# Attention logits as full-array matmuls of stacked halves, with maxima, exponentials and turned blocks taken bank by bank

## The chip, the core and the metric

The kernel runs on one core of a Trainium2 chip. The time is the device time of one execution in microseconds. The engines are TensorE (PE), VectorE (DVE), ScalarE (ACT), GpSimd (POOL) and SyncE (SP, which issues most DMAs). Each engine works through its own queue of instructions in the written order; a semaphore wait holds everything behind it on that engine.

## What is computed

A batch has 256 tokens of 256 features and 77 context rows; there are 32 batches. Four layers follow one another, each on a layer norm of x and each added to x with a gate: (a) attention without a softmax (relu of q k, relu of the result), (b) a three-layer network with weights of +1 and -1 (256 to 1024 to 1024 to 256), (c) the attention that the change is about, (d) a mixture of 64 experts with top 8 of them per token, besides a shared expert. Layer (c), cut to its core:

```python
qp = jnp.einsum('bld,ed->ble', q, Wq)
idx = jnp.argmax(jnp.einsum('bld,bmd->blm', qp, kv), axis=-1)
mem = jnp.take_along_axis(kv, idx[..., None], axis=1)
mk, mv = jnp.split(jnp.einsum('bld,ed->ble', mem, Wkv), 2, axis=-1)
qh = qp.reshape(b, l, 16, 16).transpose(0, 2, 1, 3)
attn = jax.nn.softmax(jnp.einsum('bhld,bmd->bhlm', qh, mk) / 4, axis=-1)
out = jnp.einsum('bhlm,bmd->bhld', attn, mv)
```

All 16 heads share one key and one value of 16 features. Since mem only repeats rows of the 77 context rows, the kernel takes the logits against the 77 rows, masks the rows that no token chose, and weighs values and denominator with the count of tokens that chose a row.

## The kernel before

Products that need f32 accuracy are made of f16 halves: x = high + low, and a product is high*high + high*low + low*high (`three`, L986). ACT makes the high part while it copies a result out of PSUM, DVE the low part by subtracting.

The loop over batches is a software pipeline. `body(n)` is `first(n)` and `second(n)`, written out separately for each engine, and holds work of five batches at once: layer (a) of m = n+1, layer (b) of n, layers (c) and the start of (d) of c = n-1, the rest of (d) of d = n-2, and scatters of n-3. The order of an engine's work is the order of the calls, and semaphores join the engines. After the batches a second loop runs over the 64 experts; the change doesn't touch it.

The steps that matter here:

- `b_l0`, `b_l1`, `b_l2` (L1062, L1077, L1095) are the matmuls of (b). `b_l1(0)` to `b_l1(7)` are 16 matmuls each, placed as filler between the steps of (c). ACT and DVE follow with the two halves of a result (`b_l0`, `b_l1` at L777, L783, L1576, L1579). `b_l1(0)` waits for `l0_lo` of the fourth `b_l0`.
- `c_lg(r)` (L1136), r = 0 to 3, makes the logits of 128 tokens (t) and 8 heads (half c of the features). It writes both banks of `ps_lg`, four heads of 77 columns in each. For each of four parts (the mask row, keys high with queries high, keys low with queries high, keys high with queries low) there are two matmuls, one for the upper and one for the lower 64 rows of the array. Keys lie in `kb_h`, `kb_l` as blocks of a diagonal (made by POOL in `take_keys`, L577), the mask in `mrow`.
- `c_max(r)` (DVE, L1630) takes the maxima of 8 heads at once, `c_exp(r)` (ACT, L792) eight exponentials into `p32`. `c_pt(k)` (PE, L1154) turns blocks of 128 columns of `p32`: three for even k, two for odd; ACT copies the high part, DVE the low part (L803, L1640). `c_av(r)` (L1176) multiplies with the values, `c_norm` (DVE) divides.
- There is one `p32` and one `pt_h`, `pt_l`: the exponentials of r wait until the blocks of r-1 are turned.
- `transposes(i, ...)` (L994) turns a normalised x for i = 0 to 3: `xn[0]`, `xn[1]`, `xn[2]` and, for i = 3, `xr`. All four, and `c_att`, write the same bank, `ps_tr`, so each waits for the low part of the one before it:

```python
elif i == 1:
    w(pe, tr_lo[3], b - 1)
```

- `ln_norm(1)` (ACT, L734) makes `xn[1]` from `x1`. It waits for `ln_shift(1)` of DVE (L1541), and that for a power made by POOL. In ACT's order it stands behind `tr_high(3)`, in DVE's order `ln_shift(1)` stands behind `tr_low(3)`.
- `d_gu(j)` (L1219) are the gate and up matmuls of the shared expert. They need `tr_lo[3]`.

PE's order in `second(n)` is: a_q, a_kv, c_av(3), a_vals, a_s, c_att, b_l1(6), c_wc, b_l1(7), a_sv, b_l2(0), transposes(3), b_l2(1), d_gu(0), transposes(1), d_gu(1), d_route, d_gu(2), transposes(2), d_gu(3).

Of the kernel before, what the change touches and what calls it, by code (L numbers as in the profile page):

```python
# [8 lines left out]
F16 = mybir.dt.float16  # L9
# [8 lines left out]
P = 128  # L18
# [7 lines left out]
HB = HC // 2  # L26
VW = DH + 1
# [8 lines left out]
NEG = -1e30  # L36
# [6 lines left out]
TURNED = [range(0, 3), range(3, PC)]  # L43
# [50 lines left out]
def build(nc, x, ctxT, maskT, g_xattn, g_ffn, wq0, wk0, wv0, bq0, bk0, bv0, k0, k1, k2, s0, s1, s2,  # L94
          wqT1, wkvT1, wcT1, gates_w, sgu_w, sdown_w, e_wts, out, table):
    es = ExitStack()
    with es:
# [34 lines left out]
        row0 = sb("row0", [P, P], BF16)  # L132
# [4 lines left out]
        halfmask = sb("halfmask", [P, HB])  # L137
        pad_in = sb("pad_in", [P, 1])
# [70 lines left out]
        kr_h, kr_l = sb("kr_h", [P, S2], F16), sb("kr_l", [P, S2], F16)  # L209
        kb_h, kb_l = sb("kb_h", [P, HB, S2], F16), sb("kb_l", [P, HB, S2], F16)  # L210
# [6 lines left out]
        mrow = sb("mrow", [P, HB, S2], BF16)  # L217
# [5 lines left out]
        p32 = sb("p32", [P, PC * P])  # L223
        pt_h, pt_l = sb("pt_h", [P, PC, P], F16), sb("pt_l", [P, PC, P], F16)
# [8 lines left out]
        th = sb("th", [P, IS // P, S])  # L233
        ga = sb("ga", [P, 4, S])
# [61 lines left out]
        cx_ok, kr_hi = sem("cx_ok"), sem("kr_hi")  # L296
# [4 lines left out]
        lg_rdy, z_ok, p_ok = (many(n, 4) for n in ("lg_rdy", "z_ok", "p_ok"))  # L301
# [80 lines left out]
        def _(sp):  # L382
# [45 lines left out]
            sp.wait_ge(consts2, 31)  # L428
# [76 lines left out]
        def _(pool):  # L505
# [1478 lines left out]
```

## Time and profile before

| | |
|---|---|
| median of 3 runs | 1802.12 us (1801.63 to 1804.59) |
| the profiled execution | 1800.24 us, span 1798.5 us |
| PE busy | 1672.4 us (93% of the span) |
| DVE busy | 1315.4 us (73%) |
| ACT busy | 978.5 us (54%) |
| POOL busy | 945.7 us (53%) |
| chain that ended last | PE 75%, DMA 9%, ACT 5%, issue 5%, DVE 3%, POOL 3% |

The profile shows one execution. An engine's busy time is the union of its instructions. Matmuls are pipelined and the profile models their ends, so that a start follows another after less time than one matmul seems to take; the pace of PE is read from the starts. The batches take the first 1580 us or so of the span, the experts the rest.

### The profile page before, as it was taken

How to read it: one execution, taken by the hardware profiler on the slowest of the kernel's cores; microseconds unless marked ns; L12 is line 12 of the kernel's file. 1: busy time of each engine (PE TensorE's matmuls, PEld its weight loads, DVE VectorE, ACT ScalarE, POOL GpSimd, SP SyncE). 2: the span in 40 equal slices, each digit the busy share in tenths (PEclk: the TensorE clock that was granted, in tenths of full speed). 3: DMA queues.
4: the chain of work that ended last, by engine and by line, in shares of the span. 5: the costliest groups of instructions: out<-in, count | busy, mean ns of one | idle time of the engine just before them, and what ended most of it. 6: DMA issues, size and time to landing. Idle time of an engine off the chain costs nothing.

```text
span 1798.5 us, 51473 instructions
## 1 busy us (share of the span) xinstructions
PE 1672.4 (93%) x17308; PEld 1431.1 (80%) x17308; DVE 1315.4 (73%) x4640; ACT 978.5 (54%) x2819; POOL 945.7 (53%) x1507
## 2 busy tenths in 40 slices
PE   5799999999999999999999999999999999558885
PEld 3588888888888888888888888888888887447775
DVE  6477877777777777777778877778777776546564
ACT  3455556665555555565556555555566654324443
POOL 4015555555555555555555555555555554545554
PEclk8899999999999999999999999999999999679998
DMA  7501111111000101100000000000000012148886
GB/s 221 158 15 52 45 36 39 43 46 33 26 25 23 32 15 32 31 22 22 25 28 23 28 21 14 21 23 25 18 24 21 22 52 77 50 118 208 204 204 131
DMA packets 102656, 101.12 MB, mean 56 GB/s; under 512 B 38879, under 2 KB 92073, under 8 KB 102616
## 3 DMA queue, kind: packets, MB, share of 16 engines
q1 hardware_dynamic: 68824, 81.43, 14.9%
q0 software_dynamic: 33792, 19.17, 6.1%
q8 instruction: 22, 0.36, 0.1%
q14 instruction: 18, 0.15, 0.0%
HBM read 51.63 MB, written 111.84 MB: 91 GB/s over the span
## 4 chain that ended last, share of the span: by engine, by line
PE 75%; DMA 9%; ACT 5%; issue 5%; DVE 3%; POOL 3%; POOLq 0%; SPq 0%; ACTq 0%; DVEq 0%
PE bank L1090 21%; PE bank L991 8%; DMA out<-ey,aid 7%; PE bank L1074 6%; PE ps_yo L1106 5%; PE ps_lg L1150 5%; PE ps_yo L991 4%; PE ps_m L991 4%; PE ps_tr L1017 3%; ACT p L800 3%; PE ps_pt L1165 3%; PE ps_lg L991 3%; PE ps_m L1188 2%; POOL table L615 2%; PE ps_pt L991 2%
## 5 line engine op out<-in xcount | busy, mean ns | idle before, releaser
L615 POOL DMA_INDIRECT table<-xs,slot x496 | 503.5, 1015 | 195.6 <-issue 172.5
L800 ACT ACTIVATE p<-ps_lg,rmax 128x77 f32<-128x77 f32 x1024 | 234.8, 352 | 115.7 <-DVE rmax L1638 112.9
L1090 PE MATMUL bank<-h_h,held 128*128 128x256 f16 x2048 | 265.3, 273 | 2.0 <-DVE h_l L1573 2.0
L1090 PE MATMUL bank<-h_l,held 128*128 128x256 f16 x2048 | 265.4, 273 | 0.0
L557 POOL TENSOR_TENSOR pool_pad<-pad_in 128x1 f32<-128x1 f32 x352 | 68.6, 195 | 370.2 <-PE ps_lg L1150 156.6
L1090 PEld LDWEIGHTS bank<-h_l,held 128*128 128x128 f16 x2048 | 200.4, 98 | 23.1
L1090 PEld LDWEIGHTS bank<-h_h,held 128*128 128x128 f16 x2048 | 195.3, 98 | 23.4 <-issue 1.8
L1573 DVE SCALAR_TENSOR_TENSOR h_l<-bank,h_h 128x512 f16<-128x512 f32 x256 | 175.0, 684 | 15.7 <-ACT h_h L786 10.2
L631 POOL TENSOR_TENSOR rs<-nt,minushalf 128x2 f32<-128x2 f32 x128 | 92.2, 721 | 161.9 <-DVE nt L1538 159.1
L1638 DVE TENSOR_REDUCE rmax<-ps_lg 128x8 f32<-128x616 f32 x128 | 101.8, 795 | 80.6 <-PE ps_lg L1150 80.6
L706 POOL DMA_INDIRECT out<-ey,aid x64 | 98.6, 1541 | 97.8 <-DVE aid L1919 65.0
L786 ACT ACTIVATE h_h<-bank 128x512 f16<-128x512 f32 x128 | 77.1, 602 | 122.7 <-PE bank L1090 122.7
L806 ACT ACTIVATE pt_h<-ps_pt 128x384 f16<-128x384 f32 x128 | 62.8, 490 | 110.3 <-PE ps_pt L1165 110.3
L781 ACT ACTIVATE h_h<-bank 128x512 f16<-128x512 f32 x128 | 76.4, 597 | 78.0 <-PE bank L1074 76.0
L1643 DVE TENSOR_TENSOR pt_l<-ps_pt,pt_h 128x384 f16<-128x384 f32 x128 | 70.4, 550 | 65.6 <-ACT pt_h L806 65.4
L1106 PE MATMUL ps_yo<-held,h_h 128*128 128x256 f16 x512 | 116.1, 273 | 0.1
L1106 PE MATMUL ps_yo<-held,h_l 128*128 128x256 f16 x512 | 116.0, 271 | 0.0
L1074 PE MATMUL bank<-xt_h,held 128*128 128x256 f16 x512 | 99.8, 277 | 8.0 <-DVE dn_l L1470 5.9
L1525 DVE BATCH_NORM_STATS2 stats<-x 128x6 f32<-128x256 f32 x256 | 96.2, 418 | 13.5 <-DMA x<-in_x 3.8
L1551 DVE TENSOR_TENSOR xt_l<-ps_tr,xt_h 128x512 f16<-128x512 f32 x128 | 87.8, 686 | 17.8 <-ACT xt_h L744 14.5
L1074 PE MATMUL bank<-xt_l,held 128*128 128x256 f16 x512 | 99.7, 277 | 0.0
L991 PE MATMUL bank<-xt_h,gu_h 128*128 128x256 f16 x512 | 98.2, 274 | 1.5 <-DVE ac L1727 1.5
(277 smaller groups left out, 4593.9 us busy)
## 6 DMA issues: line engine op xcount, KB each, us to landing
ew<-in_e_wts SPq DMA_DIRECT2D x48, 384.0 KB, 4.3
table<-xg SPq DMA_DIRECT2D x8, 1284.0 KB, 18.5
xg<-table SPq DMA_DIRECT2D x64, 160.5 KB, 3.6
xs<-xr SPq DMA_DIRECT2D x31, 320.0 KB, 2.6
x<-in_x SPq DMA_DIRECT2D x32, 256.0 KB, 2.7
out<-x SPq DMA_DIRECT2D x32, 256.0 KB, 2.2
table<-xs,slot POOLq DMA_INDIRECT x496
held<-in_e_wts SPq DMA_DIRECT2D x16, 384.0 KB, 4.6
```

Source lines behind the costliest of these rows:

```text
L615: g.indirect_dma_start(out=table, out_offset=bass.IndirectOffsetOnAxis(ap=slots[:, t, k:k + 1], axis=0), in_=rows[:, t, :], in_offset=None ...
L631: g.tensor_tensor(rs[i][:, :], nt[i][:, 0, :], minushalf[:, :], ALU.pow).then_inc(ln_root[i], 1)
L706: g.indirect_dma_start(out=out, out_offset=bass.IndirectOffsetOnAxis(ap=aid[u][:, 0:1], axis=0), in_=ey[u][:, :], in_offset=None, bounds_c ...
L800: ins = a.activation(p32[:, h * S2:(h + 1) * S2], ps_lg[:, h // HB, h % HB * S2:(h % HB + 1) * S2], ACT.Exp, bias=rmax[r % 2][:, h:h + 1])
L991: ins = mm(out_, s_, m_, start=(start and i == 0), stop=(stop and i == len(seq) - 1))
L1074: ins = mm(two(bank[j % 2])[:, m % 2, :], s_, m_, start=(k == 0), stop=(k == 3))
L1090: ins = mm(two(bank[j % 2])[:, m % 2, :], wb1[:, k, m * P:(m + 1) * P], hp[:, k, :], start=(i == 0 and k == 0), stop=(i == 1 and k == FK - 1))
L1106: ins = mm(two(ps_yo)[:, t, :], hp[:, k, t * P:(t + 1) * P], wb2[:, k, :], start=(i == 0 and k == 0), stop=(i == 1 and k == FK - 1))
L1150: ins = mm(ps_lg[:, g_, 0:HB * S2], row0[rows, :] if queries is None else queries[rows, c, tt], keys[rows, :, :], start=(i == 0), stop=(i ...
L1525: last = v.bn_stats(stats[i][:, t, :], src[:, t, :])
L1573: v.scalar_tensor_tensor(hl[:, 2 * j:2 * j + 2, :], two(bank[j % 2]), 0.0, hh[:, 2 * j:2 * j + 2, :], ALU.max, ALU.subtract).then_inc(lo.s ...
L1638: v.tensor_reduce(rmax[r % 2][:, :].rearrange("p (g h) -> p g h", g=2), lg, AX, ALU.max, negate=True).then_inc(z_ok.sem, 1)
```

## The change

- The three products and the mask go into one contraction over 128 rows. A new tile `qst` holds, for each pair of heads, the high queries (rows 0 to 31), the low queries (32 to 63), the high queries again (64 to 95) and a constant (96 to 127). `kst` holds the high keys twice, the low keys, and 0 or -61440 as the mask. `c_lg(i)`, i = 0 to 7, is now one bank: two matmuls of 128 rows and 154 columns. `row0`, `mrow`, `kb_h`, `kb_l` are gone.
- DVE fills rows 0 to 63 of `qst` with 16 copies a batch (`c_stack(0)`, `c_stack(1)`), ACT rows 64 to 95 with four. POOL's `take_keys` makes `kst`.
- Maxima and exponentials go by bank: eight `c_max` of four heads, eight `c_exp` of four. `p32`, `pt_h` and `pt_l` have two buffers. Even k turns two blocks, odd k three, and each waits for one bank only.
- The order of the four groups is now by half c first, then by tokens t.
- The shared expert's `th` and `ga` have two buffers instead of four.
- The calls stand in another order on PE, ACT and DVE, in both halves of the body.

The diff, cut (setup and declarations left out):

```diff
             def take_keys(b):
...
-                g.tensor_tensor(kr_l[:, :], kr32[:, :], kr_h[:, :], ALU.subtract).then_inc(handoff, 1)
-                hm = halfmask[:, :].unsqueeze(2).to_broadcast([P, HB, S2])
+                g.tensor_tensor(kr_m[:, :], kr_h[:, :], lowpart[:, 0:1].to_broadcast([P, S2]), ALU.mult).then_inc(kb_ok, 1)
+                pool.wait_ge(kb_ok, 3 * b + 1)
+                g.tensor_tensor(kr_x[:, :], kr32[:, :], kr_m[:, :], ALU.subtract).then_inc(handoff, 1)
                 pool.wait_ge(handoff, b + 1)
-                g.tensor_tensor(kb_h[:, :, :], kr_h[:, :].unsqueeze(1).to_broadcast([P, HB, S2]), hm, ALU.mult).then_inc(kb_ok, 1)
-                g.tensor_tensor(kb_l[:, :, :], kr_l[:, :].unsqueeze(1).to_broadcast([P, HB, S2]), hm, ALU.mult).then_inc(kb_ok, 1)
+                n = 3 * Q4
+                g.tensor_tensor(kst[0:n, :, :], kr_x[0:n, :].unsqueeze(1).to_broadcast([n, PH, S2]),
+                                pairmask[0:n, :].unsqueeze(2).to_broadcast([n, PH, S2]), ALU.mult).then_inc(kb_ok, 2)
```

ACT:

```diff
+            def c_stack(b):
+
+                act.wait_ge(qp_hi, b + 1)
+                w(act, lg_rdy.sem, lg_rdy.nth(7, b - 1))
+                for p in range(HP):
+                    last = a.activation(qst[2 * Q4:3 * Q4, :, p, :], qp_h[p * Q4:(p + 1) * Q4, :, :], ACT.Copy)
+                last.then_inc(qst_a, 1)
+
+            def c_exp(i, b):
+                r, g_ = divmod(i, 2)
+                act.wait_ge(z_ok.sem, z_ok.nth(i, b))
+
+                if r > 1:
+                    act.wait_ge(pt_rdy.sem, pt_rdy.nth(2 * r - 3, b))
                 else:
-                    w(act, pt_rdy.sem, pt_rdy.nth(7, b - 1))
-                for h in range(HC):
+                    w(act, pt_rdy.sem, pt_rdy.nth(2 * r + 5, b - 1))
+                for h in range(g_ * HB, (g_ + 1) * HB):
...
                 if on(n):
                     b_l0(1, n)
+                if on(c):
+                    c_stack(c)
+                if on(n):
                     b_l0(2, n)
+                    b_l0(3, n)
                 if on(d):
                     d_route(d)
...
                 if on(c):
                     c_exp(0, c)
+                    c_exp(1, c)
+                if on(n):
+                    b_l1(0, n)
```

PE:

```diff
+                for at in range(HP // 2):
+                    ins = mm(ps_lg[:, g_, at * PH * S2:(at + 1) * PH * S2], qst[:, c, g_ * (HP // 2) + at, tt], kst[:, :, :], start=True, stop=True)
                 ins.then_inc(lg_rdy.sem, 1)
...
                     d_dn(1, d)
+                if on(n):
+                    b_l1(0, n)
                 if on(c):
                     c_lg(0, c)
+                    c_lg(1, c)
+                if on(n):
+                    b_l1(1, n)
+                if on(c):
+                    c_lg(2, c)
+                    c_pt(0, c)
                     c_vb(c)
...
                 if on(n):
-                    b_l1(6, n)
+                    b_l1(7, n)
                 if on(c):
                     c_wc(c)
-                if on(n):
-                    b_l1(7, n)
                 if on(m):
                     a_sv(m)
                 if on(n):
                     b_l2(0, n)
+                    b_l2(1, n)
                 if on(c):
                     transposes(3, c, xr)
-                if on(n):
-                    b_l2(1, n)
-                if on(c):
-                    d_gu(0, c)
                 if on(m):
                     transposes(1, m, xn[1])
                 if on(c):
+                    d_gu(0, c)
                     d_gu(1, c)
                     d_route(c)
                     d_gu(2, c)
```

DVE:

```diff
+            def c_stack(c, b):
+
+                dve.wait_ge(qp_lo, b + 1)
+                w(dve, lg_rdy.sem, lg_rdy.nth(7, b - 1))
+                for p in range(HP):
+                    mine = slice(p * Q4, (p + 1) * Q4)
+                    v.tensor_copy(qst[Q4:2 * Q4, c, p, :], qp_l[mine, c, :])
+                    last = v.tensor_copy(qst[0:Q4, c, p, :], qp_h[mine, c, :])
+                last.then_inc(qst_ok, 1)
...
                 if on(c):
                     c_counts(c)
-                if on(n):
-                    b_l0(3, n)
+                    c_stack(0, c)
+                    c_max(0, c)
+                    c_max(1, c)
+                    c_values(c)
+                if on(m) and on(n):
+                    ln_first(m)
                 if on(d):
                     d_x4(d)
                 if on(c):
-                    c_max(0, c)
-                if on(m) and on(n):
-                    ln_first(m)
-                if on(c):
-                    c_max(1, c)
+                    c_max(2, c)
                     c_pt(0, c)
+                    c_max(3, c)
+                if on(n):
+                    b_l1(0, n)
+                if on(c):
+                    c_stack(1, c)
                     c_pt(1, c)
+                    c_max(4, c)
```

Between the logits the order on PE is now: c_lg(0), c_lg(1), b_l1(1), c_lg(2), c_pt(0), c_vb, b_l1(2), c_lg(3), c_pt(1), b_l1(3), transposes(0), c_lg(4), c_pt(2), b_l1(4), c_lg(5), c_pt(3), c_av(0), b_l1(5), c_lg(6), c_pt(4), c_av(1), d_cp, c_lg(7), c_pt(5), b_l1(6), c_pt(6), c_av(2), c_pt(7). DVE goes on with d_choose, c_pt(2), c_max(5), b_l1(1), tr_low(0), c_pt(3), c_norm(0), c_max(6), d_pos, c_pt(4), c_norm(1), c_max(7), c_pt(5), b_l1(2), c_pt(6), c_norm(2), c_pt(7), d_slots. In `second`, ACT and DVE keep the order of the steps around tr_high(3), ln_norm(1), tr_low(3) and ln_shift(1).

## Rows read from the trace of the kernel before

**Rows 1.** Busy time by engine in one body; columns by the first line.

```profile
core 0: us, PE busy (x) PEld busy (x) DVE busy (x) ACT busy (x) POOL busy (x), PEclk, DMA share, GB/s
917.60:964.40 46.80, 46.71 (x512) 40.21 (x510) 36.85 (x131) 27.68 (x81) 26.46 (x46) 1.00 0.08 24
```

**Rows 2.** One tile's operation on DVE: ns min/median/max, first and last start.

```profile
L1592 DVE SCALAR_TENSOR_TENSOR qp_l<-ps_m,qp_h x32: 691/692/693, 75.8 to 1530.9; 128x512 f16<-128x512 f32 x32
```

**Rows 3.** Timeline of PE: start us, us, engine, line, operation.

```profile
921.66 0.23 PE L991 MATMUL ps_tr<-cx_h,qp_l 128*128 128x77 f16 x2
921.73 0.23 PE L991 MATMUL ps_tr<-cx_h,qp_h 128*128 128x77 f16 x2
```

**Rows 4.** Timeline of PE around the first and the fourth group of logits.

```profile
925.52 0.27 PE L991 MATMUL ps_yo<-dn_h,ac_l 128*128 128x256 f16 x1
925.73 0.30 PE L1150 MATMUL ps_lg<-mrow,row 64*128 64x308 bf16 x2
...
926.36 0.47 PE L1172 MATMUL ps_tr<-vc,wide 77*128 77x34 f16 x12
...
937.79 0.18 PE L1188 MATMUL ps_m<-vb,pt_l 128*128 128x34 f16 x1
...
938.69 0.55 PE L1165 MATMUL ps_pt<-ident,p 128*128 128x128 f32 x3
```

**Rows 5.** Groups by form on DVE: count, busy us, mean ns, idle before.

```profile
L1506 DVE TENSOR_SCALAR held<-held,sg 128x2048 f16<-128x2048 f16 x1 | 0.8, 756 | 0.0
...
L1731 DVE TENSOR_TENSOR ac_l<-ac,ac_h 128x256 f16<-128x256 f32 x8 | 3.2, 418 | 0.0
```

**Rows 6.** Timeline of DVE: a maximum, first and last step of d_choose.

```profile
927.48 0.79 DVE L1638 TENSOR_REDUCE rmax<-ps_lg 128x8 f32<-128x616 f32 x1
...
933.01 0.22 DVE L1676 MAX8 e<-ex 128x8 f32<-128x64 f32 x1
...
934.32 0.48 DVE L1690 SCALAR_TENSOR_TENSOR xr<-ex,er,chosen 128x64 f32<-128x64 f32 x2
```

**Rows 7.** Timeline of ACT: a result's high part, eight exponentials.

```profile
924.33 0.60 ACT L781 ACTIVATE h_h<-bank 128x512 f16<-128x512 f32 x1 [1.55 <-PE bank L1074]
928.39 1.83 ACT L800 ACTIVATE p<-ps_lg,rmax 128x77 f32<-128x77 f32 x8 [3.46 <-DVE rmax L1638]
```

**Rows 8.** Timelines of ACT, DVE and PE around both turnings, by engine.

```profile
954.60 1.09 ACT L739 ACTIVATE xr<-x,nb,rs 128x256 f32<-128x256 f32 x2
956.22 0.60 ACT L744 ACTIVATE xt_h<-ps_tr 128x512 f16<-128x512 f32 x1 [0.53 <-PE ps_tr L1017]
957.77 1.09 ACT L739 ACTIVATE xn<-x,nb,rs 128x256 f32<-128x256 f32 x2 [0.95 <-DVE nb L1543]
...
956.85 0.69 DVE L1551 TENSOR_TENSOR xt_l<-ps_tr,xt_h 128x512 f16<-128x512 f32 x1
957.58 0.16 DVE L1543 TENSOR_TENSOR nb<-nt,rs 128x2 f32<-128x2 f32 x1
...
955.49 0.69 PE L1017 MATMUL ps_tr<-ident,xr 128*128 128x128 f32 x4
...
957.78 0.38 PE L991 MATMUL bank<-xt_h,gu_h 128*128 128x256 f16 x2
...
959.09 0.60 PE L1017 MATMUL ps_tr<-ident,xn 128*128 128x128 f32 x4
959.53 0.38 PE L991 MATMUL bank<-xt_h,gu_h 128*128 128x256 f16 x2
```

**Rows 9.** Timeline of PE in the last batch, behind the turning of xr.

```profile
1568.91 0.29 PE L991 MATMUL ps_pt<-gw_h,xt_h 128*128 128x65 f16 x2 [1.41 <-DVE xt_l L1551]
```

**Rows 10.** Busy time and granted clock in four stretches of the setup.

```profile
59.50:62.90 3.40, 0.98 (x6) 0.40 (x4) 2.24 (x11) 1.69 (x3) 0.90 (x2) 1.00 1.06 293
62.90:70.70 7.80, 1.09 (x4) 0.58 (x4) 4.07 (x4) 4.43 (x5) 0.00 (x0) 0.50 0.85 219
70.70:76.50 5.80, 5.79 (x28) 4.14 (x29) 1.92 (x3) 1.19 (x2) 0.00 (x0) 0.50 0.01 2
28.80:32.20 3.40, 3.40 (x17) 2.34 (x18) 3.17 (x5) 1.04 (x3) 0.00 (x0) 0.50 0.95 242
```

More of the change, by code:

```diff
@@ L805, in c_pt @@
                 blocks = TURNED[k % 2]
-                a.activation(pt_h[:, blocks.start:blocks.stop, :], turned(k), ACT.Copy).then_inc(pt_hi_ok.sem, 1)
+                a.activation(pt_h[k // 2 % 2][:, blocks.start:blocks.stop, :], turned(k), ACT.Copy).then_inc(pt_hi_ok.sem, 1)
             def c_vb(b):
@@ L861, in first @@
                 if on(c):
+                    c_vb(c)
+                    c_pt(0, c)
+                    c_exp(2, c)
+                    c_pt(1, c)
+                    c_exp(3, c)
                     c_pt(2, c)
[L863 to L866 removed]
                 if on(n):
                     b_l1(1, n)
+                if on(m):
+                    tr_high(0, m, xt_h[0])
                 if on(c):
[L870 removed]
+                    c_exp(4, c)
+                    c_pt(3, c)
+                    c_exp(5, c)
+                    c_pt(4, c)
+                    c_exp(6, c)
+                    c_pt(5, c)
+                    c_exp(7, c)
+                if on(n):
+                    b_l1(2, n)
+                if on(c):
                     c_pt(6, c)
@@ L1295, in first @@
                 if on(c):
+                    c_lg(4, c)
+                    c_pt(2, c)
+                if on(n):
+                    b_l1(4, n)
+                if on(c):
+                    c_lg(5, c)
+                    c_pt(3, c)
                     c_av(0, c)
-                    c_lg(2, c)
-                    c_pt(2, c)
-                    c_pt(3, c)
                 if on(n):
-                    b_l1(3, n)
+                    b_l1(5, n)
+                if on(c):
+                    c_lg(6, c)
+                    c_pt(4, c)
+                    c_av(1, c)
                 if on(d):
@@ L1304, in first @@
                 if on(c):
-                    c_av(1, c)
-                    c_lg(3, c)
-                    c_pt(4, c)
+                    c_lg(7, c)
                     c_pt(5, c)
                 if on(n):
-                    b_l1(4, n)
-                if on(c):
-                    c_av(2, c)
-                if on(n):
-                    b_l1(5, n)
+                    b_l1(6, n)
                 if on(c):
                     c_pt(6, c)
+                    c_av(2, c)
                     c_pt(7, c)
```

196 lines of the change are left out of this document (95 added, 101 removed).

## The prediction

> **What bounds the kernel now.** The busy times of one body of the loop come first, from the view by stretches: of 46.8 us TensorE (PE) is busy for 46.7, VectorE (DVE) for 36.9 and ScalarE (ACT) for 27.7, at the full clock [rows 1]. That this is a body's length shows by an operation that runs once in each: 32 of them start between 75.8 and 1530.9, 46.9 us apart on average [rows 2]. "Busy" is not yet "at its pace", since the ends of matmuls are modelled. So I go by starts: two matmuls with 77 columns take 0.07 us, 0.036 each [rows 3]; the twelve of d_gu(0) with 256 columns take 957.78 to 959.09, 0.109 each; four transposes take 959.09 to 959.53, 0.11 each [rows 8]. Counting all matmuls of a body at such paces leaves under 1 us of waits. PE works in its written order. A body gets shorter only if PE gets less to do, and longer by every wait that a new order brings in; what DVE and ACT do costs only where PE waits for it.
>
> **The logits: what is removed.** A group of c_lg is four pairs of 64-row matmuls with 308 columns. The pairs start 0.13 to 0.14 apart, so both halves of the array do run beside each other. But the last matmul before the first group starts at 925.52, its place ends at 925.63, the group starts at 925.73 and the next work at 926.36: 0.73 us. For the fourth group the sum is 937.81 to 938.69, 0.88, the last part of it a wait for the exponentials [rows 4]. The two others lie between, at 0.72 and 0.78. Four groups cost 3.1 us a body; another 0.1 goes to the first turned block, which waits for exponentials.
>
> The Trainium skill (TensorEngine Tiling (Array Packing), Key Properties) says that changing the tiling mode drains the TensorE; the 0.10 us ahead of 925.73 agrees. The same page (When to Use Tiling) says that contractions of 64 rows or fewer should be run as row tiles, which speaks against this change; here its tiles already earn their factor of two, and what the change saves is not in the tiling but in having three products (high, low and mask) in one contraction.
>
> **What is added on PE.** Eight c_lg of two matmuls with 154 columns. No row has 154; between 77 columns (0.036) and 256 (0.109) the line gives 0.067. Sixteen of them are 1.07 us. The bounds are half of the 256-column pace, 0.055, and all of it, 0.109: 0.9 to 1.75 us. Turned blocks and the sums with values keep their counts. PE gains 3.1 + 0.1 - 1.07 = 2.1 us a body, 67 us in 32 batches (bounds 45 to 70).
>
> **What is added on DVE and ACT.** c_stack puts 16 copies of 32 partitions x 256 f16 on DVE. An f16 to f16 operation of 2048 elements took 0.756 and one of 256 with an f32 source took 0.42 [rows 5]; of DVE's time each takes some 0.08 less, as the next starts before its end shows. So a copy takes 0.14 (the first row's slope) to 0.33 of DVE, together 2.3 to 5.3 us; I take 2.3, as type and place are those of the first row. The maxima, eight of 308 elements instead of four of 616 (0.79 each [rows 6]), cost 0.6 more, the mask row less. ACT gets four copies of 512 elements, about 0.53 each by its 0.60 rows [rows 7]: 2.1 us, ahead of b_l0(2). DVE then holds some 39.5 us a body. That still fits, but with less slack in the stretch of the logits. GpSimd's key steps are as many and smaller, off PE's path. The smaller th and ga buffers wait for what was done two tiles earlier: nothing, as PE's d_gu(j) waits for gu_ac(j-2) anyway. The setup edits are a few small instructions: nothing.
>
> **Order of the first half.** b_l1(0) now comes before the logits. It needs l0_lo(3): b_l0(3) ends on PE at 924.13, ACT takes it from 924.33 to 924.93 [rows 7], DVE 0.69 more, so 925.65; PE gets there at 925.64. Nothing. Then I laid out PE, ACT and DVE in the new order with these durations (a maximum 0.48, four exponentials 0.98 from the 1.83 for eight [rows 7], d_choose 1.8 from 933.01 to 934.80 [rows 6], the others as the trace has them). DVE's queue after c_lg(0) holds two maxima, c_values, ln_first, d_x4, then a maximum, a block, a maximum, b_l1(0) and the second c_stack. That copy is done 7.2 us after c_lg(0), where c_lg(4) wants it at 7.1: 0.1. With d_choose behind it, block 2, maximum 5, b_l1(1), tr_low(0), block 3 and c_norm(0) end at 12.6, where c_av(1) wants it at 12.15: 0.45. Three waits of 0.1 follow (c_pt(7) on its exponentials, c_av(3), c_att). Together 0.85 us a body; with slower copies up to 1.9, with DVE a little ahead of my layout 0. I take 0.85, 26 us in 31 bodies.
>
> **Order of the second half: the decisive edit.** Before, PE does b_l2(0), the turning of xr, b_l2(1), d_gu(0) and then the turning of xn[1]. After, b_l2(1) comes first and the two turnings stand together. Both write ps_tr, and transposes(1) waits for tr_lo[3], that is for ACT's copy and DVE's low part of the first; and DVE's ln_shift(1) and ACT's ln_norm(1), which make xn[1], are queued behind just those two. Take S, the start of the first turning: 955.49 before. ACT's copy starts at S+0.73, DVE's low part at S+1.36, nb at S+2.09, ACT's norm at S+2.28, of 1.09 us for two halves; PE turns them at S+3.60, after b_l2(1) and d_gu(0) have filled the time [rows 8]. In the new order nothing fills it: d_gu(0) also waits for tr_lo[3], and it stands behind. With xr complete at once I take 0.1 off the chain: the first half of xn[1] is there at S+2.8, the second at S+3.3, and PE goes on at S+3.5 instead of S+0.88. That is 2.6 us of wait. S itself doesn't move against its inputs: between the end of c_wc and S there were b_l1(7), a_sv and b_l2(0), now a_sv and both b_l2, which is as many matmuls; and xr was complete at 955.69, 0.2 after S [rows 8]. Against the 0.1 us that PE loses on that before, 2.5 us more in each of the 30 bodies that hold both turnings: 75 us. Bounds: 1.5 us if only tr_lo[3] counted (the wait that the end of the run shows with the same two steps is 1.41 [rows 9]), 2.9 if the norm comes late; 45 to 87. Behind it, d_gu(0) comes after the turning, so ACT's tanh delays tr_high(1); I find transposes(2) at S+7.8 and b_l0(0) at S+9.7, with waits as before.
>
> Sum: 1800.2 (the profiled execution's own time, 1.7 over its span) - 67 + 26 + 75 = 1834. The median of the runs lies 1.9 above it: 1836.
>
> **The clock.** From 59.5 to 62.9, in the setup, PE issued six matmuls, all of them transposes, and was idle for most of the time; the granted clock was 1.0 (2.4 GHz) there and 0.5 (1.2 GHz) from 62.9. Dense matmuls resumed at 70.7 and ran at 0.5 until 76.5; another time from 28.8 to 32.2 [rows 10]. So one fall costs half of 3.4 to 5.8 us, 1.7 to 2.9. In the new order a stretch of 3.5 us per body holds eight transposes and no other matmul, about what stood ahead of the fall at 62.9. Yet dense work stands on both sides of it, as it didn't there. So I expect a fall in a part of the bodies only: a third, 10 x 2.3 = 23 us (between none and all thirty, 0 to 87). Forecast 1858.
>
> The Trainium skill (TensorE: Matmul & The Clock Gate, Part 4) says that transposes don't count as PE-busy in the same way; by that the waits and both turnings are one stretch, and falls are likelier. Its table of advice in the same page names idle gaps only, by which my gap of 2.3 us would let the clock hold: the first rival, 1836.
>
> **Rivals.** (1) The clock holds: 1836. For it: the loop shows no fall; against it: the stretch without matmuls is longer than any in the loop. 0.20. (2) It falls in nearly every body, or the copies are slow: 1836 + 30 x 2.5 = 1911, or 1836 + 31 x 1.05 = 1869 with the clock up. 0.13. (3) Faster: while PE waits in the second half, DVE and ACT draw level, so the first half's waits are nil, and the turnings' wait is only the 1.5 us of tr_lo[3]: 1802 - 67 + 45 = 1780. It decides if the wait per body stays below 2.1 us. Against it: xn[1] is behind the same copy in both queues. For it: my layout of some 60 steps can err by 0.05 each. With the wait hidden altogether 1735 to 1760. 0.22. (4) Gain and waits cancel, 1802. 0.05. The matmuls of 154 columns could be slower than the line says (1.75 us): 20 us on top of any case.
>
> **How the numbers follow.** Forecast 1858, chance 0.40, own range 1842 to 1885. The range 1780 to 1900 leaves out the lower half of rival 3 and the upper of rival 2. Under 0.2% (3.6 us) a change of this kernel can't be told from none. Faster 0.22, same 0.05, slower 0.73.
>
> **What would show it.** Right: c_lg with 2 matmuls 0.067 apart and no gap ahead; 16 DVE copies of about 0.2 us; PE idle ahead of the turning of xn, some 2.2 us a body, ended by ACT's xn; granted clock below 1.0 in parts of the loop; a body of 47.7 us without a fall. Wrong: a body below 46.5, no wait ahead of xn, or DVE busy for 95% of a body.

## The result and the profile after

The changed kernel takes 1943.5 us (median of 4 runs, 1939.4 to 1944.9) where the kernel before takes 1802.5 beside it: the ratio is 1.078, 95% interval 1.077 to 1.080. It is slower, as forecast, but by 141 us and not by 56, and beyond the range.

The page of after: busy times, the chain that ended last by engine, and three groups (count, busy us, mean ns, idle us before and what ended most of it):

```profile
PE 1687.8 (87%) x16796; PEld 1429.9 (74%) x16796; DVE 1456.9 (75%) x5281; ACT 1058.7 (54%) x2947; POOL 927.7 (48%) x1508
...
PE 42%; DVE 25%; issue 12%; ACT 8%; DMA 8%; POOL 2%; DVEq 1%; SPq 0%; POOLq 0%; ACTq 0%
...
L1043 PE MATMUL ps_tr<-ident,xn 128*128 128x128 f32 x384 | 74.6, 310 | 85.6 <-ACT xn L747 74.2
...
L1681 DVE TENSOR_REDUCE rmax<-ps_lg 128x4 f32<-128x308 f32 x256 | 117.5, 469 | 18.6 <-PE ps_lg L1177 18.1
...
L1177 PE MATMUL ps_lg<-kst,qst 128*128 128x154 f16 x512 | 72.4, 234 | 45.9 <-DVE qst L1631 44.4
```

PE had 75% of the chain before and has 42% now; DVE rose from 3% to 25%. PE has fewer matmuls and is busy for longer, with more of the span idle: it waits, and in part it runs at the lower clock. The idle times of the first and the last group name the two waits: ahead of the turning of xn (ACT) and ahead of the logits (DVE's copies).

The view by stretches, two bodies and one stretch inside the first (columns as in [rows 1]):

```profile
core 0: us, PE busy (x) PEld busy (x) DVE busy (x) ACT busy (x) POOL busy (x), PEclk, DMA share, GB/s
364.27:416.21 51.94, 47.81 (x495) 40.40 (x494) 41.27 (x151) 30.15 (x85) 25.88 (x46) 0.97 0.12 37
416.21:466.68 50.47, 46.28 (x496) 39.59 (x495) 41.29 (x151) 30.14 (x85) 25.90 (x46) 1.00 0.13 41
371.70:375.10 3.40, 3.40 (x16) 2.33 (x17) 1.34 (x7) 0.33 (x1) 2.81 (x4) 0.50 0.26 95
```

A body took 46.8 us [rows 1]. It takes 50.5 with the clock up and 51.9 where it falls to 0.5 (1.2 GHz) for 3.4 us, from the second turning on; that happens in 19 of the 31 bodies of the trace. DVE is busy for 41.3 us of a body, 4.4 more than before.

What PE waited for from 262 to 1400 us, some 22 bodies (in all, times, longest):

```profile
PE ps_tr L1043 <- ACT xn L747: 48.4, 22, 3.6
PE ps_lg L1177 <- DVE qst L1631: 29.3, 44, 1.0
PE bank L1116 <- DVE h_l L1603: 4.4, 22, 0.2
PE ps_m L1213 <- DVE att L1695: 3.9, 22, 0.2
PE ps_tr L1043 <- ACT xr L747: 2.5, 2, 1.6
```

The turnings, on PE in a body with a fall and in one without, then on ACT and on DVE in the first of them. They answer to [rows 8]:

```profile
368.66 0.79 PE L1043 MATMUL ps_tr<-ident,xr 128*128 128x128 f32 x4
371.59 1.18 PE L1043 MATMUL ps_tr<-ident,xn 128*128 128x128 f32 x4 [2.13 <-ACT xn L747]
372.56 0.64 PE L1017 MATMUL bank<-xt_h,gu_h 128*128 128x256 f16 x2
...
420.60 0.79 PE L1043 MATMUL ps_tr<-ident,xr 128*128 128x128 f32 x4
423.53 0.93 PE L1043 MATMUL ps_tr<-ident,xn 128*128 128x128 f32 x4 [2.14 <-ACT xn L747]
424.29 0.38 PE L1017 MATMUL bank<-xt_h,gu_h 128*128 128x256 f16 x2
...
369.49 0.60 ACT L752 ACTIVATE xt_h<-ps_tr 128x512 f16<-128x512 f32 x1 [0.53 <-PE ps_tr L1043]
370.93 1.09 ACT L747 ACTIVATE xn<-x,nb,rs 128x256 f32<-128x256 f32 x2 [0.85 <-DVE nb L1573]
...
370.12 0.69 DVE L1581 TENSOR_TENSOR xt_l<-ps_tr,xt_h 128x512 f16<-128x512 f32 x1 [0.23 <-ACT xt_h L752]
370.73 0.16 DVE L1573 TENSOR_TENSOR nb<-nt,rs 128x2 f32<-128x2 f32 x1
```

With S = 420.60 PE goes on at S+3.69, where it went on at S+0.88 before: 2.8 us. The chain is the one of the forecast: the copy of the first turning, its low part, nb behind it in DVE's queue, then xn on ACT.

The copies, on DVE, PE and ACT of one body:

```profile
388.36 0.33 DVE L1657 TENSOR_SCALAR kst<-ps_tr 32x154 f16<-32x154 f32 x1
388.72 0.22 DVE L1630 COPY qst<-qp_l 32x256 f16<-32x256 f16 x1
388.95 0.22 DVE L1631 COPY qst<-qp_h 32x256 f16<-32x256 f16 x1
...
390.32 0.22 DVE L1631 COPY qst<-qp_h 32x256 f16<-32x256 f16 x1
...
397.06 0.22 DVE L1630 COPY qst<-qp_l 32x256 f16<-32x256 f16 x1
...
398.86 0.22 DVE L1631 COPY qst<-qp_h 32x256 f16<-32x256 f16 x1
...
390.60 0.44 PE L1177 MATMUL ps_lg<-kst,qst 128*128 128x154 f16 x4 [0.29 <-DVE qst L1631]
...
399.22 0.29 PE L1177 MATMUL ps_lg<-kst,qst 128*128 128x154 f16 x2 [1.03 <-DVE qst L1631]
...
383.84 2.54 ACT L805 ACTIVATE qst<-qp_h 32x512 f16<-32x512 f16 x4
386.41 1.08 ACT L789 ACTIVATE h_h<-bank 128x512 f16<-128x512 f32 x2
```

Eight copies hold DVE from 388.72 to 390.54 and eight more from 397.06 to 399.07: 0.23 us from start to start, a copy of 0.216 and then 13 ns until the next. Other DVE operations start before the one ahead has ended (nb at 370.73 above, xt_l ending at 370.81); these do not. c_lg(0) and c_lg(4) start just behind the eighth copy of each set.

### The profile page after: what moved, and what is told of

The parts are those of the page before. It is cut to its first block, busy times and chain, and to the rows that moved or that the text cites. A ratio compares the mean times of both kernels' runs of the same rounds, so it can differ in the third digit from the quotient of the medians.

```text
span 1943.0 us, 51786 instructions
## 1 busy us (share of the span) xinstructions
PE 1687.8 (87%) x16796; PEld 1429.9 (74%) x16796; DVE 1456.9 (75%) x5281; ACT 1058.7 (54%) x2947; POOL 927.7 (48%) x1508
## 4 chain that ended last, share of the span: by engine, by line
PE 42%; DVE 25%; issue 12%; ACT 8%; DMA 8%; POOL 2%; DVEq 1%; SPq 0%; POOLq 0%; ACTq 0%
PE bank L1017 9%; DMA out<-ey,aid 7%; PE bank L1116 6%; PE ps_yo L1132 5%; PE ps_m L1017 4%; ACT qst L805 4%; PE ps_tr L1043 3%; DVE rmax L1681 3%; DVE qst L1631 3%; PE ps_lg L1017 3%; DVE qst L1630 3%; DVE h_l L1603 3%; DVE pt_l L1687 2%; PE ps_m L1213 2%; DVE xt_l L1581 2%
## 5 line engine op out<-in xcount | busy, mean ns | idle before, releaser
L817 ACT ACTIVATE p<-ps_lg,rmax 128x77 f32<-128x77 f32 x1024 | 247.0, 338 | 175.7 <-DVE rmax L1681 171.7
L1043 PE MATMUL ps_tr<-ident,xn 128*128 128x128 f32 x384 | 74.6, 310 | 85.6 <-ACT xn L747 74.2
L1681 DVE TENSOR_REDUCE rmax<-ps_lg 128x4 f32<-128x308 f32 x256 | 117.5, 469 | 18.6 <-PE ps_lg L1177 18.1
L1043 PEld LDWEIGHTS ps_tr<-ident,xn 128*128 128x128 f32 x384 | 44.6, 149 | 105.1 <-ACT xn L747 84.2
L1769 DVE SCALAR_TENSOR_TENSOR ga<-th,bank 128x256 f32<-128x256 f32 x128 | 53.5, 418 | 79.8 <-ACT th L845 77.6
L1017 PE MATMUL bank<-xt_h,gu_h 128*128 128x256 f16 x512 | 109.8, 300 | 3.0 <-DVE ac L1771 1.6
L1177 PE MATMUL ps_lg<-kst,qst 128*128 128x154 f16 x512 | 72.4, 234 | 45.9 <-DVE qst L1631 44.4
L1017 PE MATMUL bank<-xt_l,gu_h 128*128 128x256 f16 x512 | 109.0, 298 | 0.0
L1017 PE MATMUL bank<-xt_h,gu_l 128*128 128x256 f16 x512 | 107.8, 296 | 0.0
```

The lines of the kernel that those rows point to most:

```text
L817: ins = a.activation(p32[r % 2][:, h * S2:(h + 1) * S2], ps_lg[:, g_, h % HB * S2:(h % HB + 1) * S2], ACT.Exp, bias=rmax[r % 2][:, h:h + 1])
L1017: ins = mm(out_, s_, m_, start=(start and i == 0), stop=(stop and i == len(seq) - 1))
L1043: ins = nc.tensor.transpose(two(ps_turned[i])[:, c, t * P:(t + 1) * P], src[:, t, c * P:(c + 1) * P], ident[:, :])
L1681: v.tensor_reduce(rmax[r % 2][:, g_ * HB:(g_ + 1) * HB], ps_lg[:, g_, 0:HB * S2].rearrange("p (h k) -> p h k", k=S2), AX, ALU.max, negate= ...
```

## The experiments

Each run had the kernel before beside it on its chip; ratios are against that. "Body" is the usual distance between the same matmul of two batches, with the clock up where both kinds occur.

### The order of the turnings

**e1_order_alone**: the kernel before with this order alone.

```
 b_l2(0, n)
+b_l2(1, n)
 transposes(3, c, xr)
-b_l2(1, n)
-d_gu(0, c)
 transposes(1, m, xn[1])
+d_gu(0, c)
 d_gu(1, c)
```

> The kernel before with one edit: on TensorE b_l2(1) stands ahead of transposes(3), and transposes(1) directly behind it, ahead of d_gu(0). Theory A (the new order alone makes the wait ahead of the turning of xn): the 2.4 us and 0.45 us waits at the turning of xn appear in every body although nothing else changed, 30 x 2.8 = 84 us, plus 20 to 40 us by falls of the clock: 1885 to 1925. Rival B (the wait is a result of VectorE being late from its new copies): under 20 us more, 1802 to 1822, and no fall of the clock in the loop.

Measured: 1910.2 us against 1800.6, ratio 1.061 (1.059 to 1.062). Body 49.37, with a fall of the clock 50.86. One row of PE:

```profile
315.09 0.93 PE L1017 MATMUL ps_tr<-ident,xn 128*128 128x128 f32 x4 [2.11 <-ACT xn L739]
```

Without any stacked logits the edit costs 49.37 - 46.79 = 2.58 us a body, 77 us in 30 bodies; 23 bodies with a fall at 50.86 - 49.37 = 1.49 us are 34 more, together 111 where 110 are measured. The fall is thus a consequence of this order and needs nothing of the other parts.

**e2_old_turnings**: the kernel after with the diff above undone.

> The changed kernel with one edit undone: the order b_l2(0), transposes(3), b_l2(1), d_gu(0), transposes(1) again; b_l1(7) stays ahead of c_wc. Theory A: the wait ahead of xn goes, and one of some 1.8 us ahead of xr comes, as xr is complete only 4.7 us after c_wc and 2.6 us of work stand between; no falls of the clock: 1.1 + 1.0 us less a body, about 1943 - 65 = 1878. Rival B: the waits move on by the lateness of VectorE, total within 15 us of 1943.

Measured: 1888.7, ratio 1.049 (1.047 to 1.051); body 49.59. From 262 to 1400 us PE waited for:

```profile
PE ps_tr L1043 <- ACT xr L747: 37.0, 22, 3.3
PE ps_lg L1177 <- DVE qst L1633: 30.6, 46, 1.0
```

55 us come back, 10 fewer than Theory A gave. A wait of 1.7 us a body takes the place of the removed one, now ahead of the turning of xr, because b_l1(7) no longer stands between c_wc and it. The clock fell once in these 22 bodies. The waits for the copies are untouched.

**e3_old_second_half**: e2 with b_l1(6) and b_l1(7) on PE around c_wc again, as before.

```
 first:  c_pt(5, c)
-        b_l1(6, n)
 second: c_att(c)
-        b_l1(7, n)
+        b_l1(6, n)
         c_wc(c)
+        b_l1(7, n)
```

> As the run before, and b_l1(6) and b_l1(7) are back at their old places around c_wc, so that the whole second half on TensorE is that of before. Theory A+ (filler is short: the first half of the new order needs b_l1(6) to cover exponentials and low parts): second half without waits, but 1.3 to 1.6 us more wait in the first half, around c_av(2) and the last turned blocks: 1870 to 1885. If the first half didn't need it: 1826.

Measured: 2038.7, ratio 1.131 (1.130 to 1.133), body 54.1 to 55.5. A miss by 150 us, on the wrong side. On DVE and PE:

```profile
437.56 0.69 DVE L1604 SCALAR_TENSOR_TENSOR h_l<-bank,h_h 128x512 f16<-128x512 f32 x1 [3.74 <-ACT h_h L794]
438.16 0.74 DVE L1702 SCALAR_TENSOR_TENSOR x<-ps_m,sc,x 128x512 f32<-128x512 f32 x1
...
442.29 0.95 PE L1043 MATMUL ps_tr<-ident,xr 128*128 128x128 f32 x4 [2.77 <-ACT xr L747]
```

DVE sat idle for 3.7 us in its step b_l1(3), which now needs PE's b_l1(7) behind c_wc, and c_x3, whose input PE's c_wc had finished at about 435, started at 438.16 because it stood behind it in DVE's queue.

**k1_old_second_all**: e3, with DVE's c_x3, ln_sums(3) and ln_moments(3) ahead of b_l1(3).

> e3_old_second_half (2038.7 us) with one thing more as in the kernel before: VectorE has c_x3, ln_sums(3) and ln_moments(3) ahead of b_l1(3). Theory: in e3 b_l1(3) waited on VectorE for b_l1(7), which stood behind c_wc on TensorE, and c_x3 behind it, so xr came 2.94 us late. Here that wait goes (-2.9 us a body); the waits for VectorE's pt_l at c_av(2) and c_pt(7) in the first half (1.9 us) stay, which come from b_l1(6) no longer standing between c_pt(5) and c_pt(6): 1930 to 1960 us. Rival: the order on VectorE isn't the cause, and the time stays over 2000 us.

Measured: 1893.7, ratio 1.051 (1.049 to 1.054), body 49.5. The wait ahead of xr is gone but for 2.8 us in 22 bodies, and with it the falls but for three. What is left:

```profile
PE ps_m L1213 <- DVE pt_l L1688: 22.3, 23, 1.0
PE ps_pt L1190 <- DVE pt_l L1688: 13.9, 23, 0.6
```

The cause of e3 is settled: an order on one engine that fits the old order of another. It was worth 145 us, more than I had put on it, since the falls of the clock went too (28 in the stretch from 262 to 1400 us of e3, three in k1). The new waits (1.0 and 0.6 a body) stand where b_l1(6) is missing in the first half. A filler covers one place or the other.

### The copies

**e4_no_dve_copies**: the kernel after without DVE's 16 copies, one of two elements in the place of each set. It leaves out part of the logits' operands.

> The changed kernel without VectorE's 16 copies a batch into qst (one copy of two columns stands for each eight; the logits are then not those of the reference). Theory C (the copies, 0.23 us from start to start, hold up c_lg(0) and c_lg(4)): the waits of 1.2 and 0.46 us on qst go and part of those behind them, 2.0 to 2.6 us a body: 1863 to 1881, with the wait ahead of xn unchanged at 2.4 us. Rival: the exponentials' chain takes their place, and no more than 20 us is gained.

Measured: 1879.2, ratio 1.044 (1.042 to 1.045), body 48.67. So the copies are worth 64 us in this kernel; the wait for xn stands as it was (50.5 us in 23 bodies). Of the first half's other waits, 1.5 us a body, none is gone.

**g1_copies_alone**: the kernel before with the 20 copies, into a buffer that nobody reads.

```
 ACT:  c_stack(c)       behind d_ac(3, d), b_l0(1, n)
 DVE:  c_stack(0, c)    behind b_l0(3, n), ahead of d_x4(d)
 DVE:  c_stack(1, c)    ahead of c_pt(1, c)
```

> The kernel before with the 16 copies of VectorE and the 4 of ScalarE put in at the places where the change has them (VectorE: eight ahead of the addition d_x4 and c_max(0), eight ahead of c_pt(1); ScalarE: four behind d_ac(3)), into a buffer that nobody reads. Theory C, the copies cost by the time that they hold VectorE and ScalarE (3.7 us and 2.5 us a body in the trace of after), even where no matmul waits for their result: 1825 to 1870 us. Rival, they cost only where the logits wait for them (1.66 us a body in after): within 1800 to 1815 us here, since nobody waits.

Measured: 1965.8 against 1799.1, ratio 1.093 (1.090 to 1.095), beyond what either theory gave. Waits from 262 to 1400 us:

```profile
PE ps_pt L1178 <- ACT p L810: 53.4, 22, 2.4
PE ps_m L1201 <- DVE pt_l L1664: 20.6, 33, 1.3
```

Nobody waits for a copy, and they cost 167 us: all steps of DVE behind them come late, and PE meets that at the first turned block, where the old order has only b_l1(0) and b_l1(1) as cover. The clock falls in most bodies here as well.

**g2_act_copies_alone** and **g3_dve_copies_alone**: ACT's 4 and DVE's 16 of them.

> The kernel before with ScalarE's 4 copies alone, read by nobody (g1_copies_alone without VectorE's 16). If ScalarE's copies carry much of the 163 us (they stand ahead of b_l0(2), whose bank TensorE waits for): 1840 to 1880 us. If they are small, as 0.37 us a body ahead of b_l1(0) in after suggests: 1802 to 1825 us.

> The kernel before with VectorE's 16 copies alone, read by nobody (g1_copies_alone without ScalarE's 4). All 3.7 us stand between c_counts and c_pt(1), where the kernel before has only b_l1(0) and b_l1(1) as cover: if they carry the cost of g1, 1900 to 1950 us; if they are worth what e4_no_dve_copies gave back (64 us): 1855 to 1875 us.

Measured, on a chip where the kernel before takes 1867.9: ACT's alone 1.004 (1.003 to 1.006), DVE's alone 1.066 (1.063 to 1.068). DVE's carry the cost. Whether both together lose more than the two by themselves isn't shown: g1 (1965.8, ratio 1.093) ran on a chip where the kernel before takes 1799.1, and g3 by itself took 1990.9 here.

**e5_same_partitions**: the kernel after with copies that read the partitions they write (wrong operands).

```
-v.tensor_copy(qst[Q4:2 * Q4, c, p, :], qp_l[mine, c, :])
+v.tensor_copy(qst[Q4:2 * Q4, c, p, :], qp_l[Q4:2 * Q4, c, :])
-v.tensor_copy(qst[0:Q4, c, p, :], qp_h[mine, c, :])
+v.tensor_copy(qst[0:Q4, c, p, :], qp_h[0:Q4, c, :])
```

> The kernel after, where VectorE's 16 copies read the partitions that they write (so wrong values go to the logits; sizes and counts are the same). In after such a copy takes 0.216 us and the next starts 13 ns behind its end, where other VectorE operations overlap by some 35 to 85 ns. If crossing partitions is the cause of the spacing, the copies start 0.15 us apart here and the time falls by up to 40 us; if the copy of 256 f16 itself is, they stay 0.23 us apart and the time at 1940 us.

**e6_merged_copies**: 8 copies of both halves c at once, all ahead of c_max(0).

> The kernel after with VectorE's 16 copies of 256 elements merged to 8 of 512 (both halves c at once), all ahead of c_max(0); nothing is left out. If a copy costs by its elements, 8 take 0.43 us each, 3.4 us stand ahead of c_lg(0), whose wait grows from 0.46 to about 2.1 us while the 1.2 us ahead of c_lg(4) goes: 1945 to 1965 us. If a fixed part dominates, 8 take 0.28 us each, 2.2 us: 1905 to 1925 us.

Measured, in one run each: 1943.3, no change, and 1935.9. The copies' rows (ns min/median/max), of e5, e6 and of the two-element copy of e4:

```profile
L1631 DVE COPY qst<-qp_h x256: 214/215/339, 81.1 to 1681.2; 32x256 f16<-32x256 f16 x128
```

```profile
L1631 DVE COPY qst<-qp_h x128: 280/281/355, 80.7 to 1673.5; 32x512 f16<-32x512 f16 x128
```

```profile
L1628 DVE COPY qst<-qp_h x64: 149/154/365, 80.2 to 1621.1; 32x2 f16<-32x2 f16 x64
```

Two elements take 154 ns, 256 take 215, 512 take 281: 0.15 us fixed and 0.24 to 0.26 ns an element. Reading other partitions than are written costs nothing. Why these copies start behind each other's end stays open: in e5, as in after, each copy starts in other partitions than the one ahead of it, and no run kept them the same. Merging saves 1.3 us of DVE a body, but then all stands ahead of c_lg(0), where PE waits 1.0 us instead of 0.5 while the wait ahead of c_lg(4) is gone. The body is 51.25, the clock falls in every one of the 22; that eats most of the gain.

The Trainium skill (VectorE: DVE Perf Modes, The TRN2 errata) says that an operation with an SBUF source pays a measured fixed term of about 150 cycles of the 0.96 GHz clock, whatever its size. By that the estimate for 256 elements at four a cycle is 0.22 us; the trace agrees with 0.216. My forecast took 0.14 for the whole copy, less than the 0.154 that two elements take.

### Do the two add?

**j1_neither_cause**: e2 without DVE's 16 copies (the logits' operands left out as in e4).

> The kernel after with the old order of the turnings and without VectorE's 16 copies (this leaves out part of the logits' operands). If the two causes add (55 us and 64 us): 1815 to 1835 us. If they share a part, because what one gives back is waited for at the other: 1840 us or more. Below 1802 us only if nothing but these two lost time.

Measured: 1899.9 against 1867.9, ratio 1.017 (1.015 to 1.019). From the ratios of after, e2 and e4 alone it would be 1.078 - 0.030 - 0.035 = 1.014. They nearly add, as far as ratios of different chips can tell (after, e2 and e4 ran where the kernel before takes 1801 to 1803). With both gone the kernel is still slower than before: 2.4 us a body are waited ahead of xr, and the clock falls 13 times from 262 to 1400 us. So there is a third cause, the place of the fillers b_l1, which the new order moved. It is argued from two waits: the one ahead of xr goes when b_l1(7) stands behind c_wc (k1), and others then come where b_l1(6) stood. No run gives it by itself.

### Can the stacked logits win?

**f1_copies_by_dma**: the kernel after with the 20 copies made by SyncE's queue.

```
+def stack(b):    # SyncE, as soon as qp_l is there
+    for k, q in ((1, qp_l), (0, qp_h), (2, qp_h)):
+        for p in range(HP):
+            sp.dma_start(qst[k * Q4:(k + 1) * Q4, :, p, :], q[p * Q4:(p + 1) * Q4, :, :]).then_inc(qst_in, 16)
```

> The kernel after, the 20 copies of VectorE and ScalarE replaced by 12 DMAs on SyncE's queue (each 32 partitions, both halves c), issued when qp_l is there. Nothing is left out. Theory C: VectorE gets 3.7 us a body back and ScalarE 2.5, the waits ahead of c_lg(0) and c_lg(4) go as in the run without VectorE's copies (1879 us), and the wait ahead of b_l1(0) shrinks too: 1855 to 1880 us. Rival: the transfers land later than the 6.9 us that lie between qp_l and c_lg(0) in after, and TensorE waits for them: 1900 us or more.

Measured: 2013.7, ratio 1.119 (1.116 to 1.122): the rival. SyncE, then PE:

```profile
401.15 2.60 SPq L410 DMA_DIRECT2D qst<-qp_l  x4
403.78 5.08 SPq L410 DMA_DIRECT2D qst<-qp_h  x8
...
410.19 0.44 PE L1176 MATMUL ps_lg<-kst,qst 128*128 128x154 f16 x4 [2.84 <-DMA qst<-qp_h]
```

A DMA of 32 KB takes the queue 0.65 us to issue, twelve take 7.7, and PE goes on 1.3 us behind the last.

**f2_dma_old_turnings**: f1 with the old order of the turnings.

> The run before this one (copies by DMA) with the old order of the second half's turnings on TensorE alone: b_l2(0), transposes(3), b_l2(1), d_gu(0), transposes(1). If the two causes simply add (copies, and turnings side by side, the latter worth 55 us in e2_old_turnings): 55 us under it, 1800 to 1830 us. If they share a part (the time given back by one is waited for at the other): 1830 to 1870 us.

Measured: 1947.0, ratio 1.083 (1.081 to 1.085). Against f1 67 us are won, but the level was f1's, not the one I had expected.

**f3_fillers_later**: f2 with each b_l1 one slot later on PE (none ahead of c_lg(0); b_l1(6), b_l1(7) around c_wc), ACT and DVE moved to match, and DVE's c_x3 ahead of b_l1(3).

> The run before this one, with every second-layer matmul group b_l1 one slot later (none ahead of c_lg(0), b_l1(6) and b_l1(7) around c_wc as in the kernel before), ScalarE's and VectorE's orders moved to match, and VectorE's c_x3, ln_sums(3) and ln_moments(3) ahead of b_l1(3) as in the kernel before. Theory F: e3_old_second_half lost its time by the order between the engines (c_x3 behind b_l1(3) on VectorE, 2.94 us ahead of transposes(3)) and by the missing filler between c_pt(5) and c_av(2); here both are mended, no large wait is left, and the stacked logits' shorter TensorE time shows: 1765 to 1800 us. Rival: the maxima and exponentials by bank make the first half bound by the chain lg, max, exp, turning, copies, whatever the fillers: 1820 us or more.

Measured: 1966.1, ratio 1.094 (1.092 to 1.095). But one wait holds nearly all of it:

```profile
PE ps_lg L1177 <- DMA qst<-qp_h: 102.6, 22, 4.7
PE ps_m L1213 <- DVE att L1687: 4.1, 21, 0.2
PE ps_tr L1045 <- ACT xr L758: 2.4, 2, 1.5
```

**h2_copies_spread**: f3 with the copies shared out.

```
 SyncE: 4 DMAs of qp_h (p 0, 1) behind qp_hi, 4 of qp_l behind qp_lo
 ACT:   4 copies of qp_h (p 2, 3) behind d_route, ahead of c_exp(0)
 PE:    c_lg(0), b_l1(0), c_lg(1), c_lg(2), c_pt(0), c_vb, b_l1(1)
```

> f3_fillers_later with the copies spread so that none is late: the DMAs took 0.65 us each to issue there, one after the other, and c_lg(0) waited 4.8 us a body for the twelfth. Here SyncE issues 8 of them (those of c_lg(0) and c_lg(1)'s operands first, the first four already behind qp_h), ScalarE makes 4 copies in the 3.5 us in which it idles ahead of c_exp(0), and on TensorE b_l1(0) stands between c_lg(0) and c_lg(1). All that f3 lost ahead of c_lg(0) should go, but for 0.2 us, and with it the falls of the clock: 52.17 - 4.8 - 1.0 = 46.4 us a body, 1775 to 1805 us. Rival: what was covered by that wait comes out (c_values, ln_first and d_x4 ahead of c_max(2) on VectorE): 1820 us or more.

Measured: 1830.9, ratio 1.015 (1.013 to 1.017), body 47.83, no fall in the loop. The rival: of three waits of 0.5 to 0.6 us a body by the view (0.6 to 0.7 by PE's starts) two are

```profile
PE ps_lg L1192 <- ACT p L831: 12.5, 24, 0.5
PE ps_lg L1192 <- DVE kst L1664: 10.2, 23, 0.5
```

and the third stands ahead of c_vb, for DVE's c_values.

**h3_orders_mended** and, the same kernel again, **h4_orders_again**:

```
 DVE: b_l0(2), c_counts, b_l0(3), c_max(0), c_values, c_max(1)
 PE:  c_lg(1), b_l1(1), c_lg(2), c_pt(0), c_vb, c_lg(3)
```

> h2_copies_spread (1830.9 us, 47.83 us a body) with three orders changed at the three largest waits that its trace shows: c_counts ahead of b_l0(3) on VectorE, as in the kernel before (0.58 us ahead of c_lg(0), waiting for kst); c_values between c_max(0) and c_max(1) (0.73 us ahead of c_vb); b_l1(1) between c_lg(1) and c_lg(2) on TensorE (0.68 us ahead of c_lg(2), waiting for c_exp(0)). If the loss is in the orders: 46.0 to 46.5 us a body, 1770 to 1795 us, below the kernel before. If the chain of maxima, exponentials and turned blocks by bank bounds the first half, the waits come back behind other matmuls: 1815 us or more.

> The same kernel as h3_orders_mended, beside the kernel before on one chip again. If its ratio of 0.980 holds: 1760 to 1775 us where the kernel before takes 1802; if the gain was that chip's alone: a ratio of 0.99 to 1.00.

Measured: 1829.3 against 1867.9, ratio 0.980 (0.978 to 0.982), and on another chip 1816.7 against 1847.2, ratio 0.983 (0.981 to 0.985). A body of the second:

```profile
293.48:340.30 46.82, 45.45 (x496) 39.92 (x495) 37.52 (x135) 30.48 (x85) 25.87 (x45) 1.00 0.14 43
```

With its orders put right and its copies shared out, the change is 1.7 to 2.0% faster than the kernel before on these two chips. For the others that isn't shown. On these two the kernel before took 45 and 66 us more than on the others, and no trace of it was taken there. The body of h4 is 46.8 us, no shorter than the 46.8 of [rows 1] on another chip; 0.7 us of it is a wait of PE ahead of the matmuls of `hot` (the rows that tokens chose), where the kernel before and h2 have 1.1 and 1.2 us in their whole traces. From h2 (first chips) to h3 the body went from 47.8 to 47.0 us, some 25 us or 1.4% of the time, while the ratio fell by 3.5%: the rest is a difference between the chips. On a chip where the kernel before takes 1802 the nearest figure is h2's, 1.5% slower.

**h5_addition_first**: h4 with DVE's d_x4 ahead of ln_first.

> h3_orders_mended with VectorE's addition d_x4 ahead of ln_first (the new x tile's statistics) instead of behind it: 0.68 us a body were waited ahead of c_pt(1) on TensorE until d_x4 had read its bank of PSUM. If that wait is on the path: 10 to 22 us under the run before this one. If c_max(2) behind both sets the pace: no difference beyond 3 us.

Measured: 1826.4, ratio 0.989 (0.987 to 0.991), some 10 us slower than h4: a miss. The body went from 46.8 to 47.2. PE's waits show why, first h4, then h5:

```profile
PE ps_yo L1205 <- DVE x L1791: 12.3, 24, 0.5
```

```profile
PE ps_tr L1057 <- POOL xn L664: 17.6, 24, 0.7
```

The wait for d_x4 was real and is gone. But the statistics of ln_first now stand behind it, POOL makes xn[0] from them, and PE waits for that ahead of transposes(0); its waits for DVE's att grew too, from 4.6 to 8.5 us.

## Why the prediction was right in sign and wrong in size

The forecast was 1858 and 1943.5 is measured, 85 us more. By the prediction's own terms, per body with the clock up: it had -2.1 (logits) + 0.85 (first half) + 2.5 (second half), together +1.25, which makes a body of 48.05 us (the 47.7 that it named doesn't follow from them). Measured are 50.47, +3.7. The difference of 2.4 in 31 bodies is 75 us, nearly all of what the forecast is off; 5 more are the clock's.

- **Logits on PE, -2.1: right.** c_lg has two matmuls 0.067 us apart; its share of a body is 1.07 us.
- **Second half, +2.5: right.** After shows 2.8, e1 by itself 2.58. Every step of the chain was met within 0.2 us: nb at S+2.07 (S+2.09 before), xn turned from S+2.93 (2.8), PE on at S+3.69 (3.5).
- **First half, +0.85: the step that failed.** PE waits 0.46 us ahead of c_lg(0) (forecast none), 1.20 ahead of c_lg(4) (0.1), 0.37 ahead of b_l1(0) (none, "PE gets there at 925.64") and four times 0.2 to 0.35 behind: 3.1 us. Two terms under it were mis-sized. DVE's copies take 0.23 each, 3.7 us a body and not 2.3. The 0.14 taken for a copy was called the slope of a row of 2048 elements, but 0.756 us over 2048 gives 0.094 for 256; no row gives 0.14, and a copy's fixed part alone is 0.15. An overlap of 0.08 was also taken off, which these operations do not have. The upper bound of 5.3 held it; the value taken did not. ACT's copies take 0.63 each instead of 0.53, 2.5 us, and delay h_h of b_l0(2), which I had in the list of costs ("ahead of b_l0(2)") but not in the layout; that the 0.37 us come from them is argued, not shown. 1.66 of the 3.1 us are waited for DVE's copies; the other 1.5 stay without them (e4), where the layout had 0.75. e4 gives the size in time: without DVE's copies the body is 50.47 - 48.67 = 1.8 us shorter, 56 of the 64 us that come back. g3 shows that the cost hangs on what stands around them: in the old order the same copies cost 6.6%, and PE waits up to 2.2 us a body at the first turned block.
- **The clock, +23: near in sum, wrong in both factors, so the sum is luck.** It fell in 19 of 31 bodies, not in a third, and each fall cost 51.94 - 50.47 = 1.47 us, not 2.3: 28 us. All stretches of the steady loop at 0.5 but one are 3.4 us long, as the shorter one of [rows 10]; half of that is 1.7, and the mean with the stretch of 5.8 us was too much. The likeness to the fall in the setup rested on a misreading: of the six matmuls from 59.5 to 62.9 four are transposes, the other two are ordinary ones that end there. The Trainium skill (TensorE: Matmul & The Clock Gate, Part 4) says that transposes do not count as busy in the same way. By that the two turnings and the wait between them are one stretch. The runs neither prove nor need it. The clock fell in 24 of 31 bodies in e1, where 2.1 us lie between two turnings, and once in 22 in e2, where 1.7 us are waited with b_l2(0) ahead and one turning and b_l2(1) behind. But in j1, with the order of e2 and 2.4 us of wait, it fell 13 times, and in f3 22 times around a wait of 4.7 us with no turning beside it.
- **Rivals.** Rival 2 had the right side, and both its halves: falls and slow copies. I had joined them by "or" and priced them from 1836 apart, 1911 and 1869; as both have their root in one layout they should have been one case: 1836 + 28 + 31 x 2.3 = 1935. Rival 1 (the clock holds) is out by the 19 falls. Rival 3 (DVE and ACT draw level in the second half, so that the first is free of waits) found nothing in the trace.
- **The range** ended at 1900 for want of that joint case, and because a layout by hand of some 60 steps was given an error of 0.05 each, of either sign. The errors that counted had one sign: both kinds of copies were longer than taken (maxima and exponentials came as laid out), and each set of DVE's copies ends where PE already waits for it.

## What to carry to other kernels

Price a small copy by a row of a small copy, or bound it from above and take the bound; here the fixed part is 0.15 of 0.216 us, and sixteen of them are a stage of their own on the engine. An operation that nobody waits for still delays all that stands behind it in its engine's queue: before moving or adding one, follow the queue to the next place where TensorE meets that engine, and count the matmuls that cover it there. When TensorE's order is changed, the orders of the other engines must be changed with it; one step waiting at the head of VectorE's queue (e3 against k1) was worth 145 us, as much as the whole change lost.

## What was not expected of the hardware

- DVE's f16 copies within SBUF took 154, 215 and 281 ns for 2, 256 and 512 elements, and the next started 13 ns behind the end, not before it.
- Whether they read the partitions that they write or others made no difference to them (215 ns either way, 1943.3 us).
- A DMA of 32 partitions x 1 KB within SBUF held SyncE's queue for 0.65 us; its result was used 1.3 us after the last issue had ended.
- The granted clock fell to 0.5 (1.2 GHz) in the steady loop, mostly for 3.4 us at a time and with some 1.5 us lost each. In the traces from 262 to 1400 us it fell 12 to 31 times in the kernels whose bodies hold a wait of 2.1 to 4.7 us (after, e1, e3, e4, e5, e6, f1, f2, f3, g1, g3, j1), once in e2, three times in k1, and never in before, g2 and h2 to h5.
- The kernel before took 1799 to 1803 us beside most runs, and 1847.2 and 1867.9 on two other chips; why was not looked into.
